# Self attention: the softmax weights of every second unit turned by a transposing DMA, stack DMAs issued head by head, projections in a new order

## The chip, the cores and the metric

One Trainium2 chip, of which one core runs the kernel. The metric is the device time in microseconds of one execution of the whole program. The median of three runs of the kernel before is 1657.0 us (1652.92 to 1657.8).

## The reference

One decoder layer on x (8 batches x 512 tokens x 512 channels, float32), in three parts, each added to its input:

```python
x = x + attn(layernorm(x))     # 16 heads of 32 channels, causal, q, k, v with bias, then @ Wo + bo
x = x + xattn(layernorm(x))    # 16 query heads of 128, 8 key/value heads, context 64 x 256
x = x + ffn(layernorm(x))      # gate over 8 experts, the best one: A (64 x 512), then Bw (512 x 64)

# attn, per batch and head:
scores = (q @ k.T) * 32 ** -0.5 + causal       # 512 x 512
probs = softmax(scores)
y = probs @ v
```

Only the first part, self attention, is touched by the change.

## The kernel before

The program has three stages, one after the other: `cross_products` (products of the weights and the context for the cross attention), `self_attention`, and `cross_attention_and_experts`. Inside a stage each engine runs its own list of instructions in order; semaphores connect them. There is no planner at run time: the order on every engine is written out when the program is built.

To keep float32 precision on TensorE, a value is split into a high part and a low part, and a product is three matmuls (high x high, high x low, low x high; `product`, L40 to L45). ScalarE writes the high part of a result, VectorE subtracts it and writes the low part.

Self attention works batch by batch (8). The 16 heads are 4 quads of 4 heads; a quad's q and k are 128 rows. The scores of a quad are worked off in 11 units: for the first 128 queries (i = 0) one unit with 4 heads of 128 keys, for i = 1 two units with 2 heads of 256 keys, for i = 2 four units with one head of 384 keys, for i = 3 four units with one head of 512 keys. So a batch has 44 units, and a unit's weights are at most 128 x 512. Units go in pairs: pair g holds the units 2g and 2g + 1 (the even and the odd one), 22 pairs a batch, 176 in all.

A unit passes through these steps:

- TensorE: scores from `stack` (L841), the causal mask added by a matmul (L849)
- VectorE: the negative row maxima (L732)
- ScalarE: the exponentials into `probs` (float32, in SBUF, one buffer for even and one for odd units) with their sums (L643)
- TensorE: `turn`, one transpose for each block of 128 x 128 of `probs` into PSUM (`turned`, L859): 3 or 4 blocks a unit
- ScalarE: high part `pt_hi` in float16 (L652); VectorE: low part `pt_lo` (L739)
- TensorE: `weigh`, the products with v (L878, L880)
- VectorE: sums of the three parts and reciprocals (L749, L750); GpSimd: the scaling into `y` (L597)

The loop of TensorE over the pairs g (L892 to L902) is what sets the order: turn pair g, scores and mask of pair g + 1, some steps of other products, weigh pair g - 1. "Loop g" or "the loop at 399.46" below is this loop, which begins with the first turning of pair g.

The other products are the projections q and k (`"qk"`, 8 for a batch: even numbers q, odd numbers k, two for each quad), v (`"v"`, 4), the output projection (`"o"`, 4), and the transposes of the normalised x (`"xt"`, 4) and of y (`"yt"`, 4). They are spread over the pairs by `beside_pairs` (L374): `early(b)` goes beside the first 11 pairs of batch b, `late(b)` beside the last 11, in the order written, at a rate that follows LENGTH (L371). A projection is drained by ScalarE (high part) and VectorE (low part).

The scores need q and k stacked: `stack` holds for each head q high, q high, q low against k high, k low, k high in 96 rows. SP does this with DMAs inside SBUF, 3 for each head, 12 for a quad (`stack_quad`, L531 to L541). SP waits until the k projection of the quad is drained, and until the scores of the quad two before are done, and then issues all 12. TensorE waits for all 12 before the quad's first unit (L832). SP also loads x for the LayerNorm and for the residual, and stores the output tiles (all four of a batch after the quads of the next batch are stacked).

Of the kernel before, what the change touches and what calls it, by code (L numbers as in the profile page):

```python
# [7 lines left out]
F16 = mybir.dt.float16  # L8
# [26 lines left out]
def raw(ap):  # L35

    return ap.bitcast(F32)
# [356 lines left out]
def self_attention(nc, x, self_split, bias_self, bo, x1_dram, xn, ident, vw_stored, m_dram, m_raw):  # L394
# [14 lines left out]
    def early(b):  # L409
        uses = [(b, *u) for u in (("qk", 3), ("v", 2), ("v", 3), ("qk", 4), ("qk", 5))] + [(b - 1, "yt", 3)] * (b > 0)  # L410
        return uses + [(b, "qk", 6), (b, "qk", 7)] + [(b - 1, "o", 0)] * (b > 0)

    def late(b):
        uses = [(b + 1, "xt", 0)] * (b + 1 < B)
        for t in range(1, TT):
            uses += [(b - 1, "o", t)] * (b > 0) + [(b + 1, "xt", t)] * (b + 1 < B)
        uses += [(b + 1, "qk", 0), (b + 1, "qk", 1)] * (b + 1 < B) + [(b, "yt", 0), (b, "yt", 1)]
        return uses + [(b + 1, "v", 0), (b + 1, "v", 1), (b + 1, "qk", 2)] * (b + 1 < B) + [(b, "yt", 2)]
# [5 lines left out]
    BESIDE = [steps for b in range(B) for steps in (*beside_pairs(early(b), NP // 2, 1, length(early(1))),  # L424
# [5 lines left out]
    def pairs_filling(use):  # L430
        return [g for g, uses in enumerate(FILLED) if use in uses][0]

# [4 lines left out]
    with ExitStack() as ctx:  # L437
# [35 lines left out]
        probs = sb("probs", [P, 2, T], F32)  # L473
        pt_hi, pt_lo = (sb(f"pt_{n}", [P, 4, T], F16) for n in ("hi", "lo"))
# [18 lines left out]
        y_full, y_summed, y_ready = sem("y_full"), sem("y_summed"), sem("y_ready")  # L493
# [29 lines left out]

        STACK_DMAS = 16 * 3 * HQ

        @block.sync
        def _(sp):
# [3 lines left out]
            def stack_quad(b, q):  # L531
# [5 lines left out]
                for j in range(HQ):  # L537
                    rows = slice(j * HD, (j + 1) * HD)
                    for r, (of_q, of_k) in enumerate([(Q_HI, K_HI), (Q_HI, K_LO), (Q_LO, K_HI)]):
                        sp.dma_start(raw(st[r * HD:(r + 1) * HD, :, j, :]),  # L540
                                     raw(qk[q % 2][rows, of_q:of_k + 1:of_k - of_q, :])).then_inc(stacked[q % 2], 16)  # L541
# [10 lines left out]
            stack_quad(0, 0)  # L552
            for b in range(B):
                stack_quad(b, 1)
                stack_quad(b, 2)
                stack_quad(b, 3)
                if b:
                    store_x1(b - 1, range(TT))
                    sp.wait_ge(x1_stored, b * TT * 16)
                sp.dma_start(x_res[:, :, :], x[b].rearrange("(t p) c -> p t c", p=P)).then_inc(x_res_loaded, 16)  # L560
                if b + 2 < B:
                    sp.wait_ge(gemm_drained, drained((b + 1, "xt", KT - 1)))
                    load_x(b + 2)
                if b + 1 < B:
                    stack_quad(b + 1, 0)
# [8 lines left out]
        def _(pool):  # L574
# [18 lines left out]
            for b in range(B):  # L593
                for g in range(GROUPS):
                    q, i = divmod(g, TT)
                    pool.wait_ge(y_summed, b * GROUPS + g + 1)
                    nc.gpsimd.tensor_tensor(y[:, i, q * P:(q + 1) * P].rearrange("p (h d) -> p h d", h=HQ),  # L597
                                            y_sum[:, g % 2, :].rearrange("p (h d) -> p h d", h=HQ),
                                            y_rec[:, g % 2, :].unsqueeze(2).to_broadcast([P, HQ, HD]),
                                            ALU.mult).then_inc(y_ready, 1)  # L600
                    if g == 1:
                        values_third(b, 2)
                        values_third(b, 3)
                    if g == 2 and b + 1 < B:
                        reciprocal_deviation(b + 1)
                    if g == 3 * TT:
                        pool.wait_ge(x_res_loaded, b * 16 + 16)
                        nc.gpsimd.tensor_tensor(x_res[:, :, :], x_res[:, :, :], bo_all[:, :].unsqueeze(1).to_broadcast([P, TT, D]),
                                                ALU.add).then_inc(x_res_ready, 1)
                    if g in (3 * TT + 1, 3 * TT + 2) and b + 1 < B:  # L610
                        values_third(b + 1, g - 3 * TT - 1)

        @block.scalar
        def _(act):
# [33 lines left out]
            def probs_hi(s):  # L648
                q, i, heads = UNITS[s % NU]
                width = (i + 1) * P * len(heads)  # L650
                act.wait_ge(turned_full, s + 1)
# [8 lines left out]
            for s in pair_units(0):  # L660
                exps(s)
# [897 lines left out]
```

## Time and profile before

| | us |
|---|---|
| median of three runs | 1657.0 |
| profiled execution, its own time | 1660.59 |
| its span (first to last instruction) | 1658.8 |

| engine | busy, share of the span |
|---|---|
| PE (TensorE, matmul) | 1547.3, 93% |
| PEld (TensorE, weight load) | 1289.4, 78% |
| DVE (VectorE) | 1221.4, 74% |
| ACT (ScalarE) | 831.7, 50% |
| POOL (GpSimd) | 407.7, 25% |

The mean granted clock of TensorE is 0.970 of full speed. In the span cut into 40 equal slices the line of PE is

```profile
PE   7886898999999999999999847999999999999998
```

Each digit is the busy share of a slice of 41.5 us in tenths. The first four slices are `cross_products`, the run of nines up to the 8 is self attention, the rest the last stage. Busy time is the union of the durations of an engine's instructions; since matmuls are pipelined and overlap, the duration of one is not what it adds to the time.

### The profile page before, as it was taken

The page shows a single profiled execution, that of the slowest core. Times are in us where ns is not written, and L with a number is a line of the kernel's source. Part 1 is how long each engine was busy: PE and PEld are TensorE (multiplying, and loading weights), DVE is VectorE, ACT ScalarE, POOL GpSimd, SP SyncE. Part 2 cuts the span into 40 slices and gives each one's busy share as a digit, 9 for nine tenths or more (in the row PEclk, how much of TensorE's full clock was granted, in tenths as well). Part 3 has the DMA queues.
Part 4 walks back from the last instruction along what each step waited for, and adds up shares of the span by engine and source line. Part 5 has one row for each costly group of instructions (what it writes and reads, how often), then busy time and mean ns, then how long its engine had stood idle before and what let it go on. Part 6 is the DMA issues. An engine that isn't in the chain of part 4 may idle for free. (4 is left out here: it accounts for less than half of the span.)

```text
span 1658.8 us, 29018 instructions
## 1 busy us (share of the span) xinstructions
PE 1547.3 (93%) x10720; PEld 1289.4 (78%) x10720; DVE 1221.4 (74%) x2417; ACT 831.7 (50%) x1992; POOL 407.7 (25%) x357
## 2 busy tenths in 40 slices
PE   7886898999999999999999847999999999999998
PEld 5665777888788888888888635878887887888886
DVE  4345486888888788888877757787878787878765
ACT  4443476677677776767777623232322222323211
POOL 2231112112021211202121134342424243333310
PEclk9998899999999999999999977999999999999999
DMA  9998442342444434244333424122222222222000
GB/s 320 317 320 248 106 106 62 77 129 64 105 121 88 109 77 130 62 119 112 90 78 77 140 104 159 70 77 77 77 78 82 77 77 78 77 77 83 26 14 26
DMA packets 75195, 178.95 MB, mean 108 GB/s; under 512 B 9392, under 2 KB 9520, under 8 KB 71344
## 3 DMA queue, kind: packets, MB, share of 16 engines
q1 hardware_dynamic: 75056, 177.07, 36.9%
q8 instruction: 90, 1.47, 0.4%
q14 instruction: 49, 0.40, 0.1%
HBM read 76.37 MB, written 50.33 MB: 76 GB/s over the span
## 5 line engine op out<-in xcount | busy, mean ns | idle before, releaser
L643 ACT ACTIVATE a_probs<-a_score,a_neg_max 128x384 f32<-128x384 f32 (+3 forms) x512 | 264.5, 527 | 137.4 <-DVE a_neg_max L732 136.7
L732 DVE TENSOR_REDUCE a_neg_max<-a_score 128x1 f32<-128x384 f32 (+3 forms) x352 | 208.8, 635 | 74.8 <-PE a_score L849 74.5
L652 ACT ACTIVATE a_pt_hi<-a_turned 128x512 f16<-128x512 f32 (+1 forms) x352 | 181.3, 561 | 67.7 <-PE a_turned L859 66.5
L739 DVE TENSOR_TENSOR a_pt_lo<-a_turned,a_pt_hi 128x512 f16<-128x512 f32 (+1 forms) x352 | 207.7, 631 | 0.0
L859 PE MATMUL a_turned<-ident,a_probs 128*128 128x128 f32 x1280 | 185.9, 282 | 22.8 <-DVE a_pt_lo L739 11.5
L597 POOL TENSOR_TENSOR a_y<-a_y_sum,a_y_rec 128x128 f32<-128x128 f32 x128 | 51.3, 401 | 587.7 <-DVE a_y_sum L750 585.7
L859 PEld LDWEIGHTS a_turned<-ident,a_probs 128*128 128x128 f32 x1280 | 138.0, 142 | 37.4 <-ACT a_probs L643 30.4
L1204 ACT ACTIVATE b_probs<-b_probs 128x1024 f32<-128x1024 f32 x32 | 33.9, 1060 | 197.0 <-DVE b_probs L1323 197.0
L841 PE MATMUL a_score<-a_stack 96*128 96x384 f32 (+3 forms) x512 | 126.5, 354 | 2.8 <-DMA a_stack<-a_qk 2.8
L878 PEld LDWEIGHTS a_out_y<-a_v,a_pt_hi 128*128 128x128 f16 x1280 | 97.8, 99 | 30.2 <-DVE a_pt_lo L739 14.5
L878 PE MATMUL a_out_y<-a_v,a_pt_hi 128*128 128x96 bf16 x1280 | 118.9, 210 | 1.4 <-DVE a_pt_lo L739 0.9
L44 PE MATMUL b_score<-b_m_hi,b_xt_hi 128*128 128x512 f32 x256 | 105.4, 412 | 12.7 <-DVE b_m_lo L1287 9.1
L880 PE MATMUL a_out_y<-a_v,a_pt_lo 128*128 128x64 bf16 x1280 | 115.0, 194 | 0.0
L44 PE MATMUL a_gemm<-a_xt_hi,w_self_hi 128*128 128x512 f32 x256 | 110.1, 430 | 1.2 <-DVE a_xt_lo L703 0.6
L44 PE MATMUL b_summed<-b_vw_hi,b_pt_hi 128*128 128x512 f32 x256 | 100.7, 393 | 5.5 <-DVE b_pt_lo L1239 5.5
L1130 POOL TENSOR_TENSOR b_probs<-b_probs,b_row_scale 128x1024 f32<-128x1024 f32 x32 | 61.2, 1913 | 175.2 <-DVE b_row_scale L1331 175.2
L643 ACT ACTIVATION_READ_ACCUMULATOR a_probs<-a_score,a_neg_max 128x1 f32 x512 | 103.0, 201 | 0.0
L44 PE MATMUL a_gemm<-a_xt_lo,w_self_hi 128*128 128x512 f32 x256 | 102.7, 401 | 0.0
L44 PE MATMUL a_gemm<-a_xt_hi,w_self_lo 128*128 128x512 f32 x256 | 102.5, 400 | 0.0
L44 PE MATMUL b_score<-b_m_lo,b_xt_hi 128*128 128x512 f32 x256 | 102.4, 400 | 0.0
L44 PE MATMUL b_score<-b_m_hi,b_xt_lo 128*128 128x512 f32 x256 | 101.5, 396 | 0.0
L44 PE MATMUL b_summed<-b_vw_hi,b_pt_lo 128*128 128x512 f32 x256 | 100.4, 392 | 0.0
(189 smaller groups left out, 4068.2 us busy)
## 6 DMA issues: line engine op xcount, KB each, us to landing
a_stack<-a_qk SPq DMA_DIRECT2D x384, 128.0 KB, 2.4
m_dram<-c_m_out SPq DMA_DIRECT2D x8, 2048.0 KB, 13.5
vw_dram<-shared SPq DMA_DIRECT2D x32, 512.0 KB, 8.3
shared<-m_dram SPq DMA_DIRECT2D x8, 2048.0 KB, 8.6
b_vw_raw<-vw_dram SPq DMA_DIRECT2D x8, 2048.0 KB, 8.3
c_w_raw<-w_group_dram SPq DMA_DIRECT2D x7, 1280.0 KB, 11.0
xn<-x_dram SPq DMA_DIRECT2D x8, 1024.0 KB, 5.5
a_x_res<-x_dram SPq DMA_DIRECT2D x8, 1024.0 KB, 5.2
```

Source lines behind the costliest of these rows:

```text
L44: last = nc.tensor.matmul(out, a, b, start=start and n == 0, stop=stop and n == 2)
L597: nc.gpsimd.tensor_tensor(y[:, i, q * P:(q + 1) * P].rearrange("p (h d) -> p h d", h=HQ), y_sum[:, g % 2, :].rearrange("p (h d) -> p h d", ...
L643: ins = nc.scalar.activation(probs[:, s % 2, k * width:(k + 1) * width], score[s % 2][:, k * width:(k + 1) * width], ACT.Exp, bias=neg_max ...
L652: nc.scalar.activation(pt_hi[:, s % 4, 0:width], turned[s % 2][:, 0:width], ACT.Copy).then_inc(pt_hi_ready, 1)
L732: nc.vector.tensor_reduce(neg_max[:, c:c + k], score[s % 2][:, 0:k * width].rearrange("p (h s) -> p h s", h=k), AX, ALU.max, negate=True). ...
L739: nc.vector.tensor_tensor(pt_lo[:, s % 4, 0:width], turned[s % 2][:, 0:width], pt_hi[:, s % 4, 0:width], ALU.subtract).then_inc(pt_ready, 1)
L841: nc.tensor.matmul(score[s % 2][:, at:at + width], st[:, 0, j, i * P:(i + 1) * P], st[:, 1, j, 0:width], start=k == 0, stop=False)
L859: last = nc.tensor.transpose(turned[s % 2][:, c * P:(c + 1) * P], probs[:, s % 2, c * P:(c + 1) * P], ident[:, :])
L878: nc.tensor.matmul(out_y[g % 2][:, at:at + V3], pt_hi[:, s % 4, c:c + P], val, start=t == 0, stop=False)
L880: last = nc.tensor.matmul(out_y[g % 2][:, at:at + 2 * HD], pt_lo[:, s % 4, c:c + P], val[:, 0:2 * HD], start=False, stop=t == i)
L1130: nc.gpsimd.tensor_tensor(probs[:, :, :], probs[:, :, :], row_scale[:, :].unsqueeze(2).to_broadcast([P, XH, S]), ALU.mult).then_inc(probs_ ...
L1204: nc.scalar.activation(probs[:, :, :], probs[:, :, :], ACT.Exp).then_inc(exp_ready, 1)
```

## The change

All of it is in `self_attention`.

- The odd units of all pairs but the last four (172 of 352, `BY_DMA`) are no longer turned by TensorE. ScalarE copies `probs` of the unit to float16 (`parts_hi`) right behind the pair's exponentials, GpSimd subtracts it and writes the low part beside it (`parts_lo`), and SP issues one DMA that turns high and low part together (`turn_parts`, up to 128 x 1024 of float16) into `parts_t`. There are 3 slots; they lie in the tile `shared`, which this stage left free before. `weigh` waits for the DMA and reads `parts_t`. The even units (and the last four odd ones) go as before, with their own numbering (`AMONG`).
- `exps` waits for GpSimd's low part of the unit that had the same buffer of `probs`.
- SP's list is no longer by quads but by pairs: for pair g first the turning of its odd unit, then the heads to be stacked (3 DMAs each), then stores and loads. The heads of a quad are spread evenly from the pair after its k projection is filled (`first`) to two pairs before the quad's first unit (`last`), and the fourth head is always at `last`.
- The projections come in another order: `"qk", 3` moves into the batch before, 4 and 5 ahead of v, and the output tiles and x's transposes are shifted. The lengths beside single pairs change with it, the total does not.
- Output tiles are stored one at a time as they are finished; x and bo are added by GpSimd in four pieces; the LayerNorm of the next batch is normalised two pairs earlier; the first load of the last stage waits for the last unit turned by DMA.

```diff
     def early(b):
-        uses = [(b, *u) for u in (("qk", 3), ("v", 2), ("v", 3), ("qk", 4), ("qk", 5))] + [(b - 1, "yt", 3)] * (b > 0)
-        return uses + [(b, "qk", 6), (b, "qk", 7)] + [(b - 1, "o", 0)] * (b > 0)
+        uses = [(b, "qk", 3)] * (b == 0) + [(b, *u) for u in (("qk", 4), ("qk", 5), ("v", 2), ("v", 3))]
+        uses += [(b - 1, "yt", 3)] * (b > 0) + [(b, "qk", 6), (b, "qk", 7)]
+        return uses + [(b - 1, "o", 0)] * (b > 0) + [(b + 1, "xt", 0)] * (b + 1 < B) + [(b - 1, "o", 1)] * (b > 0)
...
+        uses = [(b + 1, "xt", 1)] * (b + 1 < B) + [(b - 1, "o", 2)] * (b > 0) + [(b + 1, "xt", 2), (b + 1, "xt", 3)] * (b + 1 < B)
+        uses += [(b + 1, "qk", 0), (b + 1, "qk", 1)] * (b + 1 < B) + [(b - 1, "o", 3)] * (b > 0) + [(b, "yt", 0), (b, "yt", 1)]
+        return uses + [(b + 1, "v", 0), (b + 1, "v", 1), (b + 1, "qk", 2), (b + 1, "qk", 3)] * (b + 1 < B) + [(b, "yt", 2)]
...
+    BY_DMA = [s for s in range(B * NU - 8) if s % 2 == 1]
+    BY_PE = [s for s in range(B * NU) if s not in BY_DMA]
+    AMONG = {s: k for of in (BY_DMA, BY_PE) for k, s in enumerate(of)}
+    SLOTS = 3
...
+    STACK_BESIDE = [[] for _ in range(B * NP)]
+    for n in range(1, B * QUADS):
+        b, q = divmod(n, QUADS)
+        first, last = pairs_filling((b, "qk", 2 * q + 1)) + 1 if (b, "qk", 2 * q + 1) not in AHEAD else 0, n * PQ // 2 - 2
+        if n > 1:
+            first = max(first, ((n - 1) * PQ - 1) // 2)
+        assert first <= last
+        for j in range(HQ):
+            STACK_BESIDE[first + j * (last - first) // (HQ - 1)].append((b, q, j))
...
+        parts = m_raw[:, 0:SLOTS * T].bitcast(F16).rearrange("p (n t) -> p n t", n=SLOTS)
+        parts_t = m_raw[:, SLOTS * T:2 * SLOTS * T].bitcast(F16).rearrange("p (n c t) -> p n c t", n=SLOTS, t=P)
...
+            def turn_parts(s):
+                sp.wait_ge(parts_ready, AMONG[s] + 1)
+                if before_in_slot(s) is not None:
+                    sp.wait_ge(weighed, before_in_slot(s) + 1)
+                width = width_of(s)
+                sp.dma_start_transpose(parts_t[:, AMONG[s] % SLOTS, 0:2 * width // P, :],
+                                       parts[:, AMONG[s] % SLOTS, 0:2 * width]).then_inc(parts_turned[AMONG[s] % SLOTS], 16)
...
+            for g in range(B * NP):
+                b, at = divmod(g, NP)
+                for s in pair_units(g):
+                    if s in BY_DMA:
+                        turn_parts(s)
+                for head in STACK_BESIDE[g]:
+                    stack_head(*head)
+                for use in FILLED[g - 1] if g else []:
+                    if use[1] == "o":
+                        store_x1(use[0], [use[2]])
...
             sp.wait_ge(vw_stored, XG * 64 + 64)
+            sp.wait_ge(weighed, BY_DMA[-1] + 1)
             sp.dma_start(m_raw, m_dram[0].rearrange("p g m -> p (g m)")).then_inc(m_loaded, 16)
...
+            def parts_lo(s):
+                pool.wait_ge(parts_hi_ready, AMONG[s] + 1)
+                nc.gpsimd.tensor_tensor(part(s, 1), probs[:, s % 2, 0:width_of(s)], part(s, 0), ALU.subtract).then_inc(parts_ready, 1)
...
                 act.wait_ge(max_ready, s + 1)
+                if s - 2 in BY_DMA:
+                    act.wait_ge(parts_ready, AMONG[s - 2] + 1)
...
+            def parts_hi(s):
+                act.wait_ge(probs_ready, s + 1)
...
+                if before_in_slot(s) is not None:
+                    act.wait_ge(parts_turned[AMONG[s] % SLOTS], landed(before_in_slot(s)))
+                nc.scalar.activation(part(s, 0), probs[:, s % 2, 0:width_of(s)], ACT.Copy).then_inc(parts_hi_ready, 1)
...
             for g in range(B * NP):
                 for s in pair_units(g):
-                    turn(s)
+                    if s in BY_PE:
+                        turn(s)
```

## Rows read from the trace of the kernel before

**Rows 1.** Busy us of each engine in one window: PE, PEld, DVE, ACT, POOL, clock, DMA share.

```profile
400.00:500.00 100.00, 99.18 (x917) 83.87 (x915) 82.78 (x171) 73.28 (x204) 18.12 (x24) 1.00 0.41 99
```

**Rows 2.** Groups of lines, 300 to 900 us: busy us, mean ns, idle before, releaser.

```profile
L739 DVE TENSOR_TENSOR a_pt_lo<-a_turned,a_pt_hi 128x512 f16<-128x512 f32 (+1 forms) x274 | 161.7, 631 | 0.0
L859 PE MATMUL a_turned<-ident,a_probs 128*128 128x128 f32 x998 | 142.2, 279 | 4.3 <-ACT a_probs L643 3.7
L859 PEld LDWEIGHTS a_turned<-ident,a_probs 128*128 128x128 f32 x997 | 105.9, 141 | 13.7 <-ACT a_probs L643 8.4 <-issue 3.0
...
L878 PEld LDWEIGHTS a_out_y<-a_v,a_pt_hi 128*128 128x128 f16 x996 | 74.4, 98 | 23.4 <-DVE a_pt_lo L739 12.1 <-issue 10.2
...
L608 POOL TENSOR_TENSOR a_x_res<-a_x_res,a_bo_all 128x2048 f32<-128x2048 f32 x6 | 27.6, 4595 | 0.0
```

**Rows 3.** Timeline of the weight loads: start us, us, instruction.

```profile
399.46 0.75 PEld L859 LDWEIGHTS a_turned<-ident,a_probs 128*128 128x128 f32 x7
...
403.47 0.86 PEld L859 LDWEIGHTS a_turned<-ident,a_probs 128*128 128x128 f32 x8
404.30 0.76 PEld L841 LDWEIGHTS a_score<-a_stack 96*128 96x128 f32 x5
...
405.62 0.19 PEld L44 LDWEIGHTS a_gemm<-a_xt_hi,w_self_lo 128*128 128x128 f32 x1
405.85 0.19 PEld L44 LDWEIGHTS a_gemm<-a_xt_hi,w_self_hi 128*128 128x128 f32 x1
...
407.68 0.10 PEld L878 LDWEIGHTS a_out_y<-a_v,a_pt_hi 128*128 128x128 f16 x1
...
407.97 0.86 PEld L859 LDWEIGHTS a_turned<-ident,a_probs 128*128 128x128 f32 x8
408.80 0.30 PEld L841 LDWEIGHTS a_score<-a_stack 96*128 96x128 f32 x2
...
424.67 0.88 PEld L859 LDWEIGHTS a_turned<-ident,a_probs 128*128 128x128 f32 x8
...
428.79 0.86 PEld L859 LDWEIGHTS a_turned<-ident,a_probs 128*128 128x128 f32 x8
```

**Rows 4.** Ends of two odd exponentials (timeline), and two lines' durations (min/median/max ns).

```profile
398.70 0.19 ACT L643 ACTIVATION_READ_ACCUMULATOR a_probs<-a_score,a_neg_max 128x1 f32 x1
...
424.78 0.20 ACT L643 ACTIVATION_READ_ACCUMULATOR a_probs<-a_score,a_neg_max 128x1 f32 x1
...
L635 ACT ACTIVATE a_v<-a_v_rest x32: 622/632/633, 177.8 to 886.8; 128x512 bf16<-128x512 f32 x32
L589 POOL TENSOR_TENSOR a_v<-a_v_rest,a_v x32: 1153/1172/1176, 178.5 to 887.5; 128x512 bf16<-128x512 f32 x32
```

**Rows 5.** The stack DMAs: ns of an issue, us to landing, who waited (us, times).

```profile
L540 SPq DMA_DIRECT2D a_stack<-a_qk x384: 585/597/2177, 175.1 to 919.1; - x192
...
  PE a_score L841: 2.8, 1
...
DMA to landing us min/median/max: 2.3/2.4/4.2
```

**Rows 6.** DMA issues (KB each, median us to landing), and two in the timeline.

```profile
shared<-m_dram SPq DMA_DIRECT2D x8, 2048.0 KB, 8.6
...
x_dram<-a_x_res SPq DMA_DIRECT2D x32, 256.0 KB, 2.0
...
b_wg_raw<-w_gate_dram SPq DMA_DIRECT2D x1, 16.0 KB, 10.6
...
934.89 0.50 SPq L568 DMA_DIRECT2D shared<-m_dram  x1
975.96 0.81 SPq L1049 DMA_DIRECT2D b_x<-x_dram  x2
```

**Rows 7.** Issues on SP: start us, us (timeline), and a line's min/median/max ns.

```profile
162.48 2.11 SPq L549 DMA_DIRECT2D a_bo_all<-bo_dram  x1
...
L546 SPq DMA_DIRECT2D x_dram<-a_x_res x32: 332/338/592, 341.7 to 973.5; - x32
```

More of the change, by code:

```diff
@@ L492, in self_attention @@
         turned_full, pt_hi_ready, pt_ready = sem("turned_full"), sem("pt_hi_ready"), sem("pt_ready")
-        y_full, y_summed, y_ready = sem("y_full"), sem("y_summed"), sem("y_ready")
+        parts_hi_ready, parts_ready = sem("parts_hi_ready"), sem("parts_ready")
+        parts_turned = [sem(f"parts{n}_turned") for n in range(SLOTS)]
+        weighed, y_summed, y_ready = sem("weighed"), sem("y_summed"), sem("y_ready")
         yt_hi_ready = sem("yt_hi_ready")
@@ L522, in pair_units, with width_of, part, landed @@
             return (2 * g, 2 * g + 1) if 0 <= g < B * NP else ()
+        def width_of(s):
+            q, i, heads = UNITS[s % NU]
+            return (i + 1) * P * len(heads)
+        def part(s, lo):
+            width = width_of(s)
+            return parts[:, AMONG[s] % SLOTS, lo * width:(lo + 1) * width]
+        def landed(s):
+            return (AMONG[s] // SLOTS + 1) * 16
         STACK_DMAS = 16 * 3 * HQ
@@ L551, in _ @@
             load_x(1)
[L552 to L565, printed above, removed]
+            for j in range(HQ):
+                stack_head(0, 0, j)
+            for g in range(B * NP):
[8 more added lines that the diff above has]
+                        store_x1(use[0], [use[2]])
+                    if use[1:] == ("xt", KT - 1) and use[0] + 1 < B:
+                        sp.wait_ge(gemm_drained, drained(use))
+                        load_x(use[0] + 1)
+                if g in X_RES_AT:
+                    if b:
+                        sp.wait_ge(x1_stored, b * TT * 16)
+                    sp.dma_start(x_res[:, :, :], x[b].rearrange("(t p) c -> p t c", p=P)).then_inc(x_res_loaded, 16)
             sp.wait_ge(vw_stored, XG * 64 + 64)
+            sp.wait_ge(weighed, BY_DMA[-1] + 1)
             sp.dma_start(m_raw, m_dram[0].rearrange("p g m -> p (g m)")).then_inc(m_loaded, 16)
@@ L592, in _ @@
             values_third(0, 1)
[L593 to L611, printed above, removed]
@@ new lines, in _ @@
+            for g in range(B * NP + 2):
+                b, at = divmod(g, NP)
+                for s in pair_units(g):
+                    if s in BY_DMA:
+                        parts_lo(s)
+                for s in pair_units(g - 2):
+                    divided(s)
+                for use in FILLED[g - 1] if 0 < g <= B * NP else []:
+                    if use[1] == "v":
+                        values_third(use[0], use[2])
+                if at == 6 and b + 1 < B:
+                    reciprocal_deviation(b + 1)
+                for n, t in [(n, t) for n in range(B) for t in range(TT)]:
+                    if g == X_RES_AT[n] + 2 + t:
+                        pool.wait_ge(x_res_loaded, n * 16 + 16)
+                        nc.gpsimd.tensor_tensor(x_res[:, t, :], x_res[:, t, :], bo_all[:, :], ALU.add).then_inc(x_res_ready, 1)
@@ L669, in _ @@
                     exps(s)
+                for s in pair_units(g + 1):
+                    if s in BY_DMA:
+                        parts_hi(s)
                 for use in FILLED[g]:
@@ L855, in turn @@
                 pe.wait_ge(probs_ready, s + 1)
-                if s > 1:
-                    pe.wait_ge(pt_ready, s - 1)
+                if AMONG[s] > 1:
+                    pe.wait_ge(pt_ready, AMONG[s] - 1)
                 for c in range((i + 1) * len(heads)):
-                    last = nc.tensor.transpose(turned[s % 2][:, c * P:(c + 1) * P], probs[:, s % 2, c * P:(c + 1) * P],
+                    last = nc.tensor.transpose(turned[AMONG[s] % 2][:, c * P:(c + 1) * P], probs[:, s % 2, c * P:(c + 1) * P],
                                                ident[:, :])
@@ L866, in weigh @@
                 g = q * TT + i
-                pe.wait_ge(pt_ready, s + 1)
+                if s in BY_DMA:
+                    pe.wait_ge(parts_turned[AMONG[s] % SLOTS], landed(s))
+                else:
+                    pe.wait_ge(pt_ready, AMONG[s] + 1)
                 if heads[0] == 0:
```

79 lines of the change are left out of this document (47 added, 32 removed).

## The prediction

> **What bounds the kernel now.** I read the windows by stage first, then the groups of lines of the stage that the change touches, then the order of time inside single pairs. In the stretch 400:500 of self attention PE is busy for 99.18 of 100 us at a granted clock of 1.00, while VectorE has 83, ScalarE 73, GpSimd 18 and the DMA engines 41% [rows 1]. What leaves PE there makes the stage shorter, as long as nothing else is late. The stage is a row of 176 pairs of units, at 4.0 to 4.5 us a pair [rows 3]. Waits of PE inside it are small: its weight loads waited 8.4 us in 600 for the probabilities and 12.1 for the low parts, and for the stacks nobody waited there (once, 2.8 us, in the whole run) [rows 2, 5].
>
> **What a turned block costs PE.** The rows offer three numbers for one transpose: its mean duration of 279 ns, its share of busy time of 142.2 us over 998, and its pitch [rows 2]. Matmuls overlap, so only the pitch is given back: eight weight loads for the turning begin at 407.97 and the next work at 408.80, and the eight before that at 403.47 and 404.30 [rows 3]. That is 0.83 us for 8, 104 ns each. Two quads (22 units) hold 80 blocks, and the odd units have 40 of them (18 in an even quad, 22 in an odd one); eight batches give 640, less 14 of the last four odd units, which stay on PE: 626. So PE gives back 626 x 0.104 = 65.1 us, 0.42 us in a pair whose odd unit has four blocks.
>
> The row shows 279 ns for an instruction and 104 ns between two. The Trainium skill, page "TensorE: Matmul & The Clock Gate", Part 4, gives about 275 ns for a transpose in a kernel's context; as a duration the trace agrees. Taken as the price it would make the gain 626 x 0.275 = 172 us, which the pitch rules out.
>
> **What the other engines get.** ScalarE writes one high part for each unit as before (0.63 us by L635, which reads SBUF as the new ones do [rows 4]), so that nothing is added to it. VectorE loses 172 low parts of 0.631 us (108 us), GpSimd gets them: 1.17 us each by its row with the same shape, at most 201 us on an engine that is 18% busy [rows 2, 4]. Both lie beside PE: free. If GpSimd were late, ScalarE would stand at the exponentials two units on, which come about 1.5 us later than GpSimd is done in the pair worked out below. The four pieces of x + bias on GpSimd are 4.6/4 = 1.15 us each and lie in pairs of their own: nothing. LayerNorm two pairs earlier, and each output tile's store on its own, have the whole stage as cover: nothing. The order of the projections changes no count of matmuls. The load of the first products into the shared tile now waits for a unit weighed four pairs before the end; it began at 934.89 and takes 8.6 us, and the next stage issues its first load at 975.96, so some 20 us cover the delay of some 15 [rows 6].
>
> **The transposing DMA.** No row of before has one. It moves up to 256 KB from SBUF to SBUF. Nearest rows: a store of 256 KB lands in 2.0 us [rows 6], a stack DMA (SBUF to SBUF, 128 KB) in 2.4 us, with an issue on SP of 0.597 us median [rows 5]. Far ends: a load of 16 KB in pieces of 128 bytes took 10.6 us to land, one issue took 2.11 us, and the shortest 0.33 [rows 6, 7]. I take 0.6 us of issue and 2.4 us to landing, since both ends are in SBUF as with the stacks.
> When is it needed? Take the pair whose loop begins at 399.46. Its odd exponential is done at 398.89. Then come 0.63 (high part), 1.17 (low part) and some 0.1 of semaphores: 400.79, that is 1.33 us into its loop [rows 3, 4]. The weighing of the odd unit came 4.2 us into the next loop (407.68), and does so 0.42 earlier now; the loop itself is 4.01 - 0.42 = 3.6 us. Deadline 3.6 + 3.8 = 7.4, so the transfer has 6.0 us and takes about 2.4. Covered, with 3.6 us to spare. Beyond 6.0 us each further us lengthens each pair by a third of it, since mask, exponential, parts, turning and weighing span three loops.
>
> The rows above give 2.4 us for such a move. The Trainium skill, page "VectorE: DVE Perf Modes", section "The three transpose paths", puts one 128 x 128 block through the DMA crossbar at 1309 ns; no run here shows it. If a unit's eight blocks (high and low) went one after the other, that is an estimate of 10.5 us, far over the cover; the page's own rule beside it, that the crossbar keeps about 90% of DMA bandwidth, says the contrary. It is the third rival in another form, priced there from rows.
>
> **SP's queue, the place where something comes due.** Before, a quad's 12 stack DMAs were issued in one go as soon as its projections were drained (12 x 0.6 = 7.2 us) [rows 5], pairs ahead of their use. Now SP goes pair by pair: it waits for the parts of the odd unit, issues the turning, then the three DMAs of a head. The last head of a quad is always put two pairs before the quad's first unit, whose scores PE starts one loop later. So it is late by this sum. Loop at 399.46: SP passes its wait at 1.33; plus 0.6 (turning), plus two issues before the last (1.2), plus 2.4 to landing: 5.5. PE wants the stack at 3.6 + 0.5 = 4.1 (scores came 0.83 into the loop, less 0.42; the quad begins with the second unit of the pair, +0.1). PE waits 1.4 us, and nothing hides it. The other kind, loop at 424.67: the odd exponential ends only at 424.98, so the parts are ready at 2.2, the last stack lands at 6.4; PE's loop was 4.12, loses 0.42, and by the new order has four matmuls of 512 columns (0.235 us each by their pitch) less to do beside: about 2.8, which the exponentials hold to 3.0 [rows 3, 4]. PE waits about 3.0. Of the four quads of a batch the other two follow loops with 9 and 12 such matmuls beside: 1.5 and 0.4 us. Mean 1.6; I take off 0.1, because a pause of PE lets late exponentials catch up: 1.5 us x 31 quads = 46.5 us. With the shortest issue (0.33 us) it is 38, with 2.11 us 31 x 3.0 = 93; if parts are ready 1.5 us earlier than I think, nothing.
> SP's load: 48 stack issues x 0.6 + 21.5 turnings x 0.6 + about 4 = 46 us a batch of some 89: no bound until a turning takes 2.6 us.
>
> **The sum.** The profiled execution took 1660.6 us (span 1658.8 and 1.8 around it). 1660.6 - 65.1 + 46.5 = 1642.0. The median of the runs, 1657.0, is 3.6 below the profiled one, so the prediction is 1638.4, said as 1638.
>
> **Rivals.**
> 1. The stacks come in time. For it: 0.597 us is the only issue price for a move within SBUF, and before nobody waited for a stack; SP might pass its waits earlier, since ScalarE no longer has the odd unit's high part ahead of the exponentials. Against: the order on SP is fixed, and so is the distance of two pairs. The whole 65.1 comes: 1592, to 1585 if late exponentials also go.
> 2. The side of slower: SP is late with the stacks by more. Mechanism: a turning's issue keeps SP longer than a plain one, and every us of it delays the last head and PE's first scores of a quad. It decides from 65.1/31 = 2.1 us of wait a quad, that is an issue of 1.2 us. With 2.11 us the waits are 93: 1657 - 65 + 93 = 1685. For it: an issue of 2.11 us exists, and the longest of a stack DMA is 2.18 [rows 5, 7]. Against: the median of a stack DMA is 0.6.
> 3. The turned parts land late. From 6.0 us to landing on. With the 10.6 us of [rows 6] each pair is (10.6 - 6.0)/3 = 1.5 us longer: 172 x 1.5 = 264, less 65: 1856; with 8.3 us, halfway between 6.0 and 10.6, 1724. For it: pieces are short. Against: 172 x 256 KB is little beside a DMA share of 41%.
> 4. It does nothing: PE has less to do, but the pairs go by the chain score, maximum, exponentials, and PE waits for that instead (ScalarE 73% now, some 80% in a stage shorter by 65 of 770 us): 1657. Against: in 600 us that chain kept PE's loads waiting 8.4 us only [rows 2].
>
> **Chances.** Forecast 38% (own range 1610 to 1656), rival 1 26%, rival 2 18%, rival 3 10%, rival 4 8%. A measurement of this kernel tells 0.3% (5 us) from no change. Faster: 0.34 of the forecast and rival 1, 0.60. Same: 0.03 and most of rival 4, 0.10. Slower: 0.30. The range takes in rival 1 to 1586 and rival 2 to 1705 and leaves out rival 3.
>
> **What would show it.** PE's turning falls to 654 blocks and its pitch stays 104 ns. PE waits for the stack DMAs some 31 times, 46 us in all; no such waits is rival 1. SP's row of the turning: issue 0.6 us; over 1.2 is rival 2. PE waiting at the weighing (L878 or L880) for the turned parts is rival 3. The idle time of PE before the turning, released by ScalarE's exponentials, above 40 us is rival 4. The forecast is wrong outright if the time is below 1610 or above 1656.

## The result: slower by 8%

The changed kernel takes 1789.75 us (median of four, 1786.78 to 1791.87) against 1656.08 before: ratio 1.0808, 95% interval 1.0784 to 1.0833. Forecast were 1638 us, wrong outright above 1656, with a range that took in the first two rivals from 1586 to 1705. The windows of the whole stage, from the first turning to the last weighing, before and then after, in the columns of [rows 1]:

```profile
188.00:959.00 771.00, 747.90 (x6877) 632.12 (x6877) 618.30 (x1253) 553.89 (x1550) 128.77 (x172) 0.98 0.39 96
```

```profile
187.00:1087.00 900.00, 748.68 (x6252) 616.46 (x6252) 526.84 (x1083) 569.19 (x1548) 314.92 (x368) 0.91 0.62 128
```

The stage grew by 129 us; the other stages are as before. PE has 625 instructions fewer and is busy just as long, and its idle time (the stage's length less its busy time) went from 23 to 151 us. No engine is full: the stage is now bound by waits. Which ones, the waits of PE's weight loads in the stage tell (us in total, times, longest), first before, then after:

```profile
PEld a_turned L859 <- ACT a_probs L643: 30.4, 47, 2.4
...
PEld a_gemm L44 <- DVE a_qk L711: 1.7, 6, 0.3
```

```profile
PEld a_score L923 <- DMA a_stack<-a_qk: 79.4, 26, 5.6
PEld a_turned L941 <- ACT a_probs L711: 42.0, 47, 2.4
...
PEld a_gemm L44 <- DVE a_xt_lo L786: 21.5, 13, 2.3
...
PEld a_gemm L44 <- DVE a_v_rest L801: 10.5, 8, 1.5
PEld a_gemm L44 <- DVE a_yt_lo L789: 7.5, 6, 1.2
PEld a_out_y L967 <- DMA shared<-shared: 6.6, 8, 1.5
```

The stacks come first, with 79 us in 26 waits, 3.1 us each, where one wait of 2.8 us stood [rows 5]. The drains of the projections' banks (xt_lo, v_rest, yt_lo) are new as well, 40 us. For the turned parts themselves PE hardly waits: 6.6 us. GpSimd's low parts take 1.16 us (median), as forecast, no wait of ScalarE for GpSimd stands in the trace, and VectorE's instructions beside them take what they took (the maxima of 128x512 0.68 us before and after), so GpSimd's new work slows neither. The turning and stacking on SP (min/median/max ns of an issue, then us to landing of the transposing DMA):

```profile
L587 SPq DMA_TRANSPOSE shared<-shared x172: 1212/1247/2307, 189.6 to 1072.4; - x172
...
DMA to landing us min/median/max: 2.7/3.1/7.4
```

One late stack in order of time, the third quad of batch 2, whose loop of PE before it begins at 464.81 (SP's and PE's timeline):

```profile
464.52 1.23 SPq L587 DMA_TRANSPOSE shared<-shared  x1
465.85 1.87 SPq L579 DMA_DIRECT2D a_stack<-a_qk  x3
```

```profile
463.40 0.19 PEld L44 LDWEIGHTS a_gemm<-w_self_hi,a_yt_lo 128*128 128x128 f32 x1
...
464.81 0.42 PEld L941 LDWEIGHTS a_turned<-ident,a_probs 128*128 128x128 f32 x4
469.74 1.35 PEld L923 LDWEIGHTS a_score<-a_stack 96*128 96x128 f32 x6 [4.51 <-DMA a_stack<-a_qk]
471.18 0.60 PEld L931 LDWEIGHTS a_score<-a_causal_bf,a_ident_bf 128*128 128x128 bf16 x6
471.74 0.34 PEld L44 LDWEIGHTS a_gemm<-w_self_hi,a_yt_hi 128*128 128x128 f32 x1
```

SP has just got the parts of its pair, when PE is already at the next pair; it issues the turning, then the head's three DMAs, and PE stands for 4.5 us. And behind the pause the weight loads of L44 take 0.34 us, where those before it took 0.19: the granted clock has gone to its lower level (1.2 GHz; 0.5 in the records). The windows show it fall while PE waits and come back some 5 us after PE has its work again, though PE is then busy all the time (the last column but two is the clock):

```profile
468.00:470.00 2.00, 0.26 (x1) 0.26 (x2) 0.00 (x0) 0.00 (x0) 0.31 (x1) 0.54 0.97 199
...
472.00:474.00 2.00, 2.00 (x6) 1.61 (x6) 1.76 (x3) 1.40 (x9) 0.00 (x0) 0.50 0.67 185
...
476.00:478.00 2.00, 2.00 (x30) 1.75 (x29) 0.74 (x2) 0.54 (x1) 0.92 (x1) 1.00 0.00 0
```

The granted clock of the stage was 0.98 and is 0.91.

### The profile page after: what moved, and what is told of

It is laid out like the page before. It is cut to its first block and busy times, and to the rows that moved or that the text cites. A ratio compares the mean times of both kernels' runs of the same rounds, so it can differ in the third digit from the quotient of the medians.

```text
span 1786.7 us, 28416 instructions
## 1 busy us (share of the span) xinstructions
PE 1544.5 (86%) x10094; PEld 1272.6 (71%) x10094; DVE 1129.6 (63%) x2245; ACT 847.5 (47%) x1992; POOL 593.1 (33%) x553
## 2 busy tenths in 40 slices
DMA packets 240938, 219.66 MB, mean 123 GB/s; under 512 B 175152, under 2 KB 175280, under 8 KB 237104
## 5 line engine op out<-in xcount | busy, mean ns | idle before, releaser
L649 POOL TENSOR_TENSOR shared<-a_probs,shared 128x512 f16<-128x512 f32 (+1 forms) x172 | 184.6, 1073 | 456.7 <-ACT shared L728 456.7
L923 PE MATMUL a_score<-a_stack 96*128 96x384 f32 (+3 forms) x512 | 145.9, 389 | 76.1 <-DMA a_stack<-a_qk 75.0
L923 PEld LDWEIGHTS a_score<-a_stack 96*128 96x128 f32 x512 | 86.2, 216 | 90.5 <-DMA a_stack<-a_qk 79.4
L941 PE MATMUL a_turned<-ident,a_probs 128*128 128x128 f32 x654 | 111.9, 292 | 35.3 <-ACT a_probs L711 32.6
L44 PE MATMUL a_gemm<-a_xt_hi,w_self_hi 128*128 128x512 f32 x256 | 115.7, 452 | 29.1 <-DVE a_xt_lo L786 17.6
L719 ACT ACTIVATE a_pt_hi<-a_turned 128x512 f16<-128x512 f32 (+1 forms) x180 | 99.2, 552 | 39.2 <-PE a_turned L941 39.0
L44 PE MATMUL b_score<-b_m_hi,b_xt_hi 128*128 128x512 f32 x256 | 105.4, 412 | 12.7 <-DVE b_m_lo L1376 9.0
L820 DVE TENSOR_TENSOR a_pt_lo<-a_turned,a_pt_hi 128x512 f16<-128x512 f32 (+1 forms) x180 | 113.4, 632 | 0.0
L44 PE MATMUL a_gemm<-a_xt_lo,w_self_hi 128*128 128x512 f32 x256 | 107.2, 419 | 0.0
L44 PE MATMUL a_gemm<-a_xt_hi,w_self_lo 128*128 128x512 f32 x256 | 107.2, 419 | 0.0
L44 PE MATMUL b_summed<-b_vw_hi,b_pt_hi 128*128 128x512 f32 x256 | 100.6, 393 | 5.5 <-DVE b_pt_lo L1328 5.5
L728 ACT ACTIVATE shared<-a_probs 128x512 f16<-128x512 f32 (+1 forms) x172 | 101.8, 592 | 5.4
L941 PEld LDWEIGHTS a_turned<-ident,a_probs 128*128 128x128 f32 x654 | 71.2, 145 | 43.9 <-ACT a_probs L711 42.0
L44 PE MATMUL b_score<-b_m_lo,b_xt_hi 128*128 128x512 f32 x256 | 102.0, 398 | 0.0
L44 PE MATMUL b_score<-b_m_hi,b_xt_lo 128*128 128x512 f32 x256 | 101.4, 396 | 0.0
L1189 POOL TENSOR_TENSOR b_rstd<-b_var,b_minus_half 128x1 f32<-128x1 f32 x64 | 35.3, 551 | 197.3 <-DVE b_var L1341 197.2
L44 PE MATMUL b_summed<-b_vw_lo,b_pt_hi 128*128 128x512 f32 x256 | 100.3, 392 | 0.0
```

The costliest lines, as they stand in the source:

```text
L44: last = nc.tensor.matmul(out, a, b, start=start and n == 0, stop=stop and n == 2)
L649: nc.gpsimd.tensor_tensor(part(s, 1), probs[:, s % 2, 0:width_of(s)], part(s, 0), ALU.subtract).then_inc(parts_ready, 1)
L719: nc.scalar.activation(pt_hi[:, AMONG[s] % 4, 0:width], turned[AMONG[s] % 2][:, 0:width], ACT.Copy).then_inc(pt_hi_ready, 1)
L728: nc.scalar.activation(part(s, 0), probs[:, s % 2, 0:width_of(s)], ACT.Copy).then_inc(parts_hi_ready, 1)
L820: nc.vector.tensor_tensor(pt_lo[:, AMONG[s] % 4, 0:width], turned[AMONG[s] % 2][:, 0:width], pt_hi[:, AMONG[s] % 4, 0:width], ALU.subtract ...
L923: nc.tensor.matmul(score[s % 2][:, at:at + width], st[:, 0, j, i * P:(i + 1) * P], st[:, 1, j, 0:width], start=k == 0, stop=False)
```

## The experiments

Times are medians of four or more runs, each beside the kernel before on the same chip (1654.8 to 1657.6 us); ratios are to it, with 95% intervals. "Stage" is the window from first turning to last weighing, idle its length less PE's busy time. The runs are called e1 to e15 in what follows.

**Stacks one pair sooner (e1)**

```diff
-        first, last = ... , n * PQ // 2 - 2
+        first, last = ... , n * PQ // 2 - 3
```

> The changed kernel with each quad's heads stacked by three pairs before its first unit instead of two. Theory S (SP is late with the last head: PE waits 79 us for the stacks in 31 places, and its pauses bring stretches at the lower clock): the waits for the stack DMAs fall under 10 us, the clock in self attention is back near 1.00, time 1595 to 1630 us. Rival T (the transposing DMA itself is late or slows everything): nothing but the place of the waits changes, 1750 us or more. Rival O (the new order of the projections leaves some pairs too little and others too much): the stack waits go, but 1690 us or more stays.

1694.78 us, 1.0253 (1.0208 to 1.0299): 95 us come back by one digit. The waits for the stacks fall from 79 to 7 us:

```profile
185.00:991.00 806.00, 701.63 (x6251) 574.42 (x6251) 522.43 (x1081) 567.02 (x1550) 315.20 (x368) 0.98 0.69 143
...
PEld a_turned L941 <- ACT a_probs L711: 53.2, 62, 3.2
...
PEld a_score L923 <- ACT a_probs L711: 12.8, 37, 0.7
...
PEld a_score L923 <- DMA a_stack<-a_qk: 7.3, 9, 1.2
```

The same 6251 matmuls are busy for 701.6 us instead of 748.7, at 0.98 instead of 0.91: 47 us of the 94 are the clock, the other 47 are idle time (151 to 104). So the mechanism of S is shown: late stacks, and the clock behind them. Its time is missed by 65 us (1595 to 1630 forecast); what rival O said, that the waits go and 1690 us or more stays, is what came.

**Nothing turned by DMA (e2)**

```diff
-    BY_DMA = [s for s in range(B * NU - 8) if s % 2 == 1]
+    BY_DMA = []
```

> The changed kernel with no unit turned by DMA: TensorE turns all 352, the new order of projections, the stacking head by head and the single stores stay. S and T: SP has no wait for parts in its list any more and runs ahead, no stack wait, so as the kernel before, 1650 to 1665 us. O: the order alone costs, 1690 us or more.

1687.07 us, 1.0196 (1.0159 to 1.0233). Between both forecasts, and nearly at O's. There is no wait for a stack in its trace.

**Heads ahead of the turning (e3)**

```diff
+                for head in STACK_BESIDE[g]:
+                    stack_head(*head)
                 for s in pair_units(g):
                     if s in BY_DMA:
                         turn_parts(s)
-                for head in STACK_BESIDE[g]:
-                    stack_head(*head)
```

> The changed kernel with SP issuing the heads of a pair ahead of the turning of that pair, not behind it. S: the last head goes out some 1.25 us (one turning) plus the wait for the parts sooner, stack waits under 15 us, the turning has enough spare time to go 1.8 us later, 1600 to 1640 us. T: 1760 us or more. O: 1690 us or more.

1694.99 us, 1.0240 (1.0203 to 1.0276), waits for the stacks 1.6 us. The same cure by another edit, and the same rest.

**A plain DMA instead of the transposing one (e4)**

```diff
-                sp.dma_start_transpose(parts_t[:, ...], parts[:, ...])
+                sp.dma_start(parts_t[:, ...], parts[:, ...].rearrange("p (c t) -> p c t", t=P))
```

> The changed kernel with a plain copying DMA of the same bytes in place of each transposing one; the weights are not turned, so the odd units' outputs are other numbers. S: an issue costs SP 0.35 to 0.6 us in place of 1.25, so the stack waits fall by 31 x 0.65 to 0.9 = 20 to 28 us and the time to 1735 to 1765 us: most of the loss stays, since the order on SP is what counts. T: the transposing is the cause, 1600 to 1640 us. O: as S.

1752.67 us, 1.0579 (1.0539 to 1.0620): 37 us less, within S's range. An issue takes 0.523 instead of 1.247 us, with landing in 2.3 instead of 3.1. The waits for stacks are 55 instead of 79 us, the 20 to 28 less that S forecast; PE's busy time falls as well, from 748.7 to 729.9 us, with the clock at 0.94 instead of 0.91. T as the main cause falls.

**The turning with the old order of projections (e5)**

```diff
     def early(b): ...      # and late(b), front: as in the kernel before
-        first, last = ... , n * PQ // 2 - 2
+        first, last = ... , n * PQ // 2 - 3
```

> The changed kernel with the heads stacked three pairs ahead and the projections in the order of the kernel before. Theory S+O (three losses that add: late stacks with the low clock behind them 94 us, the new order some 30, and the rest of PE's waits): against the 1695 us of the run with stacks sooner and the new order, 25 to 35 us less, 1660 to 1670 us. Rival (the order costs only where PE turns all units, since there PE has no idle time): 1690 us or more.

1701.17 us, 1.0276 (1.0255 to 1.0298). A miss: the old order does not help the turning, and the rival's time (1690 us or more) is what came. PE waits 21 us for the stacks again and the clock is 0.94. A likely reason is that the old order has two of the k projections later, so that heads have fewer pairs to be stacked in; no run tests it.

**Drains ahead of the high part (e6)**

```diff
+                for use in FILLED[g]:
+                    high_part(use)
                 for s in pair_units(g + 1):
                     if s in BY_DMA:
                         parts_hi(s)
-                for use in FILLED[g]:
-                    high_part(use)
```

> The run with the old order and the heads three pairs ahead, and on ScalarE the drains of the projections ahead of the odd unit's high part. Theory D (the 0.6 us of the high part delay the drain of the projections, and PE waits for that): PE's waits for a_gemm's drains (some 40 us with the new order) fall under 20 us and the time is 15 to 25 us under the run without this edit. Rival C (the chain of score, maximum and exponentials in pairs with little beside is what PE waits for): within 6 us of it.

1704.82 us, 1.0297 (1.0277 to 1.0317). D falls and C's time holds: PE's waits for drains got shorter (qk from 17.8 to 11.9 us), those for the turned parts longer (11.8 to 30.4 us at L968).

**Nothing turned by DMA, old order (e7)**

`BY_DMA = []` as in e2, and `early` and `late` of the kernel before.

> The changed kernel with nothing turned by DMA and the old order of the projections: what is left of the change is SP's list by pairs, single stores, the residual in four pieces. O: the order made all of the 30 us that the run with nothing turned by DMA lost, so 1650 to 1662 us. Rival (SP's list or the other moved pieces cost): 1675 us or more.

1660.98 us, 1.0040 (1.0025 to 1.0054). So SP's list by pairs, single stores and pieces cost 0.4%, and the new order with PE turning all 1.0196 - 1.0040 = 1.6%, 26 us. The trace of e2 has waits for xt_lo (10.8 us) that e7 has not, and more waits for exponentials (45.4 instead of 33.4 us); PE is also busy for 755.3 instead of 746.9 us there, at the same clock (0.99) and with the same number of matmuls.

**A late stack in the kernel before (e8)**

```diff
                     for r, (of_q, of_k) in enumerate(...):
+                        if b * QUADS + q > 0 and j == HQ - 1 and r == 2:
+                            sp.wait_ge(turned_full, 2 * ((b * QUADS + q) * PQ // 2 - 1) + 1)
                         sp.dma_start(...)
```

> The kernel before, with the last stack DMA of each quad from the second on held until the even unit of the pair before the quad's first is turned: no transposing DMA, no new order, only a late stack. It lands about 3.1 us into PE's loop, and PE wants it 0.8 us in: 31 waits of some 2.3 us, 71 us in all. Theory S with the clock: the pauses bring stretches at the lower clock, over 100 us of them, so 1657 + 71 + 30 to 50 = 1755 to 1780 us. Rival (a pause costs itself and no more): 1720 to 1735 us.

1738.01 us, 1.0495 (1.0468 to 1.0522): 83 us, between the two forecasts and nearer to the rival's. The wait (from 200 to 1000 us; 68 us in 31 waits over the whole stage) and the window of the stage:

```profile
PEld a_score L843 <- DMA a_stack<-a_qk: 66.0, 30, 3.2
...
188.00:1042.00 854.00, 772.94 (x6878) 649.00 (x6879) 619.78 (x1255) 555.30 (x1550) 128.24 (x172) 0.96 0.35 87
```

Idle time is up by 58 us (23 to 81), and the same number of matmuls (but one) is busy 25 us longer, at 0.96. A pause of PE of 2.2 us costs itself and some 0.4 of itself in clock. With nothing of the change in it, this kernel shows the late stacks and the clock behind them by themselves; the rest of the loss it does not show.

**Maxima ahead of the outputs (e9)**

```diff
+                for s in pair_units(g + 1):
+                    row_max(s)
                 for s in pair_units(g - 2):
                     outputs(s)
-                for s in pair_units(g + 1):
-                    row_max(s)
```

What asks for it is a pair of the run with stacks sooner. ScalarE, VectorE and the next turning of PE there, from the exponentials of one pair to those of the next:

```profile
528.23 0.58 ACT L711 ACTIVATE a_probs<-a_score,a_neg_max 128x384 f32<-128x384 f32 x1 [3.31 <-DVE a_neg_max L814]
...
528.80 0.57 ACT L711 ACTIVATE a_probs<-a_score,a_neg_max 128x384 f32<-128x384 f32 x1
...
529.49 0.52 ACT L728 ACTIVATE shared<-a_probs 128x384 f16<-128x384 f32 x1
529.92 0.67 ACT L693 ACTIVATE a_qk<-a_gemm,a_bias_q 128x512 fp32r<-128x512 f32 x1
530.49 0.48 ACT L719 ACTIVATE a_pt_hi<-a_turned 128x384 f16<-128x384 f32 x1
533.39 0.58 ACT L711 ACTIVATE a_probs<-a_score,a_neg_max 128x384 f32<-128x384 f32 x1 [2.42 <-DVE a_neg_max L814]
...
530.62 0.75 DVE L794 SCALAR_TENSOR_TENSOR a_qk<-a_gemm,a_bias_q,a_qk 128x512 fp32r<-128x512 f32 x1 [1.37 <-ACT a_qk L693]
531.29 0.54 DVE L778 TENSOR_SCALAR xn<-xn,a_moments,a_rstd 128x512 f32<-128x512 f32 x1
...
531.83 0.53 DVE L831 TENSOR_REDUCE a_y_sum<-a_out_y 128x128 f32<-128x384 f32 x1
...
532.80 1.01 DVE L814 TENSOR_REDUCE a_neg_max<-a_score 128x1 f32<-128x384 f32 x2
...
534.11 0.31 PEld L941 LDWEIGHTS a_turned<-ident,a_probs 128*128 128x128 f32 x3 [1.01 <-ACT a_probs L711]
```

Neither is full, each waits for the other in turn: exponentials, new high part (L728), drain (L693), its low part (L794), normalising, outputs, only then the maxima, whose scores had been there since about 530, then exponentials. One turn of this ring (a chain of waits that comes back to where it began) is 5.2 us here, from the even exponential at 528.23 to the next at 533.39. PE's own work in the pair is less: it stands 1.0 us for the exponentials.

> The changed kernel with the heads three pairs ahead (1695 us) and on VectorE the row maxima of the next pair ahead of the outputs of the pair before the last. Theory R (a ring of lists: the exponentials and the new high part stand on ScalarE ahead of a projection's drain, VectorE's low part of it, the normalising and the outputs stand ahead of the next maxima, and those ahead of the next exponentials; one turn of it takes 4.8 to 5.1 us, more than PE's pair): the ring gets 0.5 to 1.2 us shorter, PE's waits for the exponentials fall from 51 us to under 25, time 1660 to 1675 us. Rival (the exponentials are late for ScalarE's own load): 1690 us or more.

1668.37 us, 1.0070 (1.0046 to 1.0095), 26 us less than without. PE's waits for the exponentials before the turning fell from 53.2 to 24.5 us; those for the stacks rose from 7.3 to 13.6. Time and waits are as R said, so R is shown for this kernel.

**All of it with the old order, heads first (e10)**

> Old order of the projections, heads three pairs ahead and ahead of the turning, row maxima first; half the units turned by DMA as in the change. R with S and O: all named losses are mended, so the turning's gain of 65 us shows in part: 1615 to 1645 us, faster than the kernel before. Rival (turning by DMA brings nothing that this kernel can use): 1655 us or more.

1731.87 us, 1.0447 (1.0414 to 1.0481), a plain miss, on the side of the rival. SP stood at a head's wait for its projection with the turning queued behind it (SP for L795: 73.1 us), and PE at the weighing:

```profile
PEld a_out_y L968 <- DMA shared<-shared: 67.1, 28, 4.4
```

**Maxima first in the kernel before (e11)**

> The kernel before with the row maxima ahead of the outputs on VectorE, nothing else. R: there PE is the bound and the ring has room, so little: 1645 to 1658 us. Rival (the edit is a gain by itself, whatever turns the units): under 1640 us.

1663.92 us, 1.0037 (1.0019 to 1.0054): 6 us above R's range: no gain where the ring is not the bound, but a little loss, which R did not foresee.

**Filler ahead of the stack's wait (e12)**

```diff
-                if n % PQ == 0:
-                    pe.wait_ge(stacked[q % 2], (b * 2 + q // 2 + 1) * STACK_DMAS)
                 if s > 1:
                     pe.wait_ge(probs_ready, s - 1)
+                if n % PQ == 0:
+                    for k in range(8 if s > 1 else 0):
+                        nc.tensor.matmul(score[s % 2][:, :], w_hi[:, 0, 0:P], w_hi[:, 0, 0:T], start=True, stop=True)
+                    pe.wait_ge(stacked[q % 2], (b * 2 + q // 2 + 1) * STACK_DMAS)
```

The wait for the stack also changes places with the one for `probs_ready`; PE has to pass both anyway.

> The changed kernel with eight matmuls of 512 columns, whose result is thrown away, on PE ahead of its wait for each quad's stack (1.9 us of work in a wait of 2.5). Theory S with the clock: PE has no long pause there, the lower clock goes from 158 us of the stage to under 90 and the time from 1790 to 1745 to 1770 us. Rival (the clock does not hang on these pauses): 1785 us or more, and where the stack comes sooner than the filler ends it costs.

1767.93 us, 1.0684 (1.0644 to 1.0723): 22 us faster with 248 matmuls more. Clock of the stage 0.97 instead of 0.91:

```profile
185.00:1067.00 882.00, 768.01 (x6500) 626.70 (x6501) 526.70 (x1083) 567.00 (x1548) 314.56 (x368) 0.97 0.64 130
```

An estimate: at the 0.235 us that the prediction took for a matmul of 512 columns the filler makes 58 us, so the other matmuls are busy for some 710 us, against 748.7 without the filler and 701.6 with the stacks in time (e1). Of the clock's 47 us some 8 are left, and the filler's own time falls for the larger part into waits that were there anyway (idle 151 to 114 us). So the clock hangs on these pauses.

**Three for the rest of the gain:** maxima first and drains first in the new order (e13); the old order, heads three pairs ahead, with maxima first and the turning first on SP (e14); and this last with each low part of a drain behind the next maxima (e15).

> New order, heads three pairs ahead, row maxima first (1668 us), and on ScalarE the projections' drain ahead of the odd unit's high part. Theory R (the high part stands in the ring): the ring loses 0.5 us more, PE's waits for drains and exponentials (65 us together) fall under 45, 1650 to 1660 us. Rival L (what is taken from the ring comes back as later turned parts, as with the old order, where this edit brought nothing): 1665 us or more, with PE's waits for the turned parts over 15 us.

1667.22 us, 1.0065 (1.0041 to 1.0089), as without the drain's edit (e9). Waits for drains fell, those for the turned parts (17.4 us) and stacks (21.4 us) rose: L, give and take.

> Old order, heads three pairs ahead, row maxima first, but the turning ahead of the heads in SP's list again. Theory: the 1732 us of the run with heads first came from SP, which stood at a head's wait for its projection's drain with the turning behind it (PE then waited 67 us for turned parts). So those waits fall under 20 us, and the time to 1660 to 1690 us. Rival (the old order with the turning is slow in any list of SP): 1715 us or more.

1696.20 us, 1.0232 (1.0202 to 1.0261). The waits for turned parts are 14 us instead of 67: SP's list was the cause there. The time is a little over the forecast. Against e5, which differs in the maxima alone, it is only 5 us less; the same move gave 26 us in the new order. So with the old order something else binds: PE waits 24 us for stacks and 19 us for the drains of q and k, and the clock is 0.94.

> The run before it, and on VectorE the low part of a projection one pair later, behind the next row maxima. Theory R: the ring from exponentials over high part, drain and maxima back to the exponentials is cut, PE's waits for the exponentials fall under 10 us, 1630 to 1655 us. Rival L (the later drain makes PE, SP and the stacks wait instead): 1670 us or more, with the waits for drained banks and stacks over 40 us.

1858.93 us, 1.1223 (1.1186 to 1.1261), the slowest, and as rival L said. The waits for exponentials did not fall below 10 us either (34.6 over the stage), and drained banks and y were late (49.5 for x_res, 34.7 for qk, 30.9 for y); the clock is 0.90. Moving a wait in a list of two engines that feed each other is not cutting it.

No version tried beats the kernel before.

## Why the prediction was wrong

In the profile the stage grew by 129 us, where the sum had it 65.1 - 46.5 = 18.6 us shorter. The steps that failed are these: the pauses for the stacks were taken at 46.5 us and measured 79.4; the clock behind them was put at nothing and cost 47 us; and what ScalarE and VectorE do beside PE was called free, while their ring of waits was longer than the pair that PE had left, so that the time taken from PE came back as idle time.

By the ratios the 134 us of the whole split on one path like this: 0.4% (some 7 us) for the list by pairs and the pieces (e7), 1.6% (26 us) for the new order with PE turning all (e2 less e7), 0.6% (9 us) for the turning with stacks in time (e1 less e2, which differ in the distance of the heads too; the waits for stacks are 7 us in e1 and none in e2), 5.5% (92 us) for the stacks two pairs ahead (after less e1). Another path gives other shares: with the old order the turning costs 2.4% (e5 less e7, with 21 us of waits for stacks in e5), and the new order then costs nothing (e1 less e5: -0.2%). Both paths share their first and last step; what lies between, 2.1% or 35 us, is order and turning together.

- **The 65 us given back by PE.** The blocks fell to 654 as said, and the pitch is about what it was: four loads in 0.39 us (499.99 to 500.38). In the stage the busy time went from 755 us (e2, all turned by PE, clock 0.99) to 702 (e1, clock 0.98), 53 us instead of 65. That is real work gone, but the stage did not shorten with it.
- **The stacks' lateness.** The place and the mechanism were right: SP's order makes the last head late, in 26 waits of the 31 forecast. The size was not: 3.1 us a wait instead of 1.5. The issue of a turning was taken as 0.6 us by the stack DMA's row and is 1.247; that was rival 2, which decides from 1.2 us and by its own sum gives 31 x (1.5 + 0.65) = 67 us. And the sort of quad whose pair is short waits 4.5 to 5.6 us in batches 1 to 6, not 3.0: in the case shown SP passed its wait 2.5 us into the loop (it begins at 461.98), not 2.2, and that loop had 2.8 us, not 3.0. With 67 us of pauses in its sum the prediction would have said 1659 us, no change.
- **The clock, the step that was missing.** A pause was priced at its own length. After pauses the clock stays at its lower level for a while: 47 us in the changed kernel (busy 748.7 against 701.6 for the same matmuls), 25 us in the kernel before with a late stack alone. With the measured waits and this term in it the forecast's sum would have come to 1660.6 - 65.1 + 79 + 47 = 1722, by the profiled execution, which took 1788.5; some 67 us are still missing, and the next two points are what is left for them. The terms do not simply add: while PE stands for a stack, it does not stand for other things (e1 has 72 us less of these waits and 47 us less idle time).
- **"The order of the projections changes no count of matmuls": nothing.** Wrong by 26 us where PE turns all (e2 less e7); in the kernel with the turning no run shows a loss by it. The count is right. In e2 the waits for xt_lo are some 11 us of it, later exponentials 12, and a longer busy time for the same matmuls 8. That the new order lets a product begin while what it reads is still being drained, and that it fills pairs unevenly, are the reasons argued; they were not tested one by one.
- **"Nothing is added to ScalarE": free.** Busy time was argued where position counts. The high part used to come after a wait of its own; it now stands ahead of the drain, inside the ring of ScalarE and VectorE. In a pair with a drain the ring takes some 5 us, against 3.6 us of PE's work that I counted. So the 53 us of work taken from PE turned into 58 us of idle time (46.7 in e2, 104.4 in e1): 35 us more of waits for drains (xt_lo, v_rest, yt_lo, qk), 21 more for exponentials, and 13 for stacks and turned parts, less some shorter ones. That is rival 4 in part, to which I gave 8%, since in [rows 2] that chain kept PE waiting for 8.4 us only; it had the exponentials and not the drains. Its sign, over 40 us of waits for exponentials before the turning, came (42.0) but says little, since over the whole stage there were 30.4 before. A wait that is small because PE comes last says nothing of how close the second comes; cutting the ring by one move gave 26 us back in the new order (e9). That moving the high part alone gives nothing (e6, e13) leaves open how much of the ring's loss is its own.
- **Cover of the turned parts.** Right: 6.0 us of room, 3.1 us to landing, 6.6 us of waits in all. The crossbar's price on the page "VectorE: DVE Perf Modes" of the Trainium skill, section "The three transpose paths" (1309 ns a block), taken eight times in a row, would be an estimated 10.5 us for a unit; the trace has 3.1 for all eight blocks, so eight blocks in one DMA do not cost that much each. Rival 3 falls as a cause in this kernel; PE waits long for turned parts only in an order with SP standing at another wait (e10).

What stays open: which of the unevenness and the early drains makes how much of the 26 us of the new order, what binds the turning with the old order, and whether any order lets the turning's gain through; the best of the versions tried with it takes 1667 us.

## What to carry to other kernels

An in-order queue turns "issue it two steps ahead" into "issue it after whatever stands before it two steps ahead"; when a wait for late work is put at the head of a queue, the times of all that is behind it must be summed anew, up to the landing. Before work is taken from the engine that is full, work out the period of the next ring of waits, by following two engines' lists around once, not by their busy shares. And price a pause of TensorE at more than its length: here the lower clock behind the pauses added some 0.4 us for each us of them in the kernel before (25 for 58 us of idle time, e8), and 0.65 in the changed kernel (47 us for 72 us of waits, after against e1).

## What the runs showed of the hardware

- A transposing DMA of up to 128 x 1024 float16 inside SBUF holds SP's queue for 1.247 us, a plain DMA of the same bytes 0.523 us; they land after 3.1 and 2.3 us. It moves in small packets: 175152 under 512 bytes in the run instead of 9392 before, 12144 with the plain copy. The DMA share of the stage is 0.62 instead of 0.39, and 0.49 with the plain copy.
- Thirty-one pauses of PE of 2.2 us each, in a stage otherwise full, took the granted clock from 0.98 to 0.96 and 25 us beside the 58 of added idle time (e8). After a pause of 4.5 us in the changed kernel the clock was at 0.5 for some 5 us of full work; filling such pauses with matmuls that compute nothing made the changed kernel 22 us faster.
